# Edge tiles of 121 rows instead of 125, ids transposed on the chip, and another order of TensorE's products in the mixer of a graph layer

## The reference, cut to what matters

```python
xn = layernorm(x)
# graph attention: el, er (N, 8) are logits of source and target, feat_v (N, 8, 64) the values
e = leaky_relu(el[src] + er[dst], 0.2)
a = softmax of e over the edges of each dst (segment max, exp, segment sum)
gnn[dst] += a * feat_v[src]                       # segment sum over 100000 edges
# mixer: linear attention with positive random features
q, k, v = heads(xn @ Wq)/8, heads(xn @ Wk)/8, heads(xn @ Wv)
phi(t) = max(exp(-|t|^2/2), 1e-8) * exp(min(t @ omega, 50))
mix = (phi(q) @ (phi(k).T @ v)) / (phi(q) @ sum phi(k)) @ Wo
x1 = x + gnn + mix
# routed part: gates, 8 Sinkhorn rounds, top 781 rows of each of 8 experts, one product each
out = x1 + combine(experts(layernorm(x1)))
```

## Time and profile before

| | us |
|---|---|
| median of three runs | 3183.67 (3181.99 to 3190.54) |
| the profiled execution | 3169.73 |
| its span | 3167.7 |
| TensorE busy | 2547.4 (80%) |
| GpSimd busy | 2208.5 (70%) |
| VectorE busy | 1620.6 (51%) |
| ScalarE busy | 992.5 (31%) |
| mean granted TensorE clock | 0.92 of full speed |

### The profile page before, as it was taken

One profiled execution on the slowest core, in us unless ns is written; L12 is line 12 of the kernel. 1 busy time (PEld: TensorE's weight loads), 2 busy tenths in 40 slices (PEclk: granted clock), 3 DMA queues, 4 the chain that ended last, 5 costly groups with the idle time before them and its releaser, 6 DMA issues.

```text
span 3167.7 us, 47560 instructions
## 1 busy us (share of the span) xinstructions
PE 2547.4 (80%) x10463; PEld 1775.2 (56%) x10464; DVE 1620.6 (51%) x2963; ACT 992.5 (31%) x2564; POOL 2208.5 (70%) x1847
## 2 busy tenths in 40 slices
PE   6699999999999979941776777777788888824998
PEld 3377766667766644421554556666666666723443
DVE  6622222222222279986744555565666666767232
ACT  2322222222222200020544545554555556600111
POOL 6477777877777877787877777777777777500454
PEclk9899999999999999975799999998999999956999
DMA  6531111111111133321666677777777777630111
GB/s 162 143 81 30 29 29 30 32 29 29 29 29 29 24 118 115 115 57 24 164 173 175 178 184 182 179 183 175 188 189 195 192 194 200 174 110 0 45 52 39
DMA packets 276634, 341.25 MB, mean 108 GB/s; under 512 B 165456, under 2 KB 184631, under 8 KB 276451
## 3 DMA queue, kind: packets, MB, share of 16 engines
q0 software_dynamic: 218672, 227.51, 32.0%
q1 hardware_dynamic: 52093, 93.57, 9.4%
q10 hardware_dynamic: 5810, 19.52, 2.0%
HBM read 285.65 MB, written 55.25 MB: 108 GB/s over the span
## 4 chain that ended last, share of the span: by engine, by line
POOL 41%; issue 16%; PE 15%; DMA 14%; DVE 9%; DVEq 3%; POOLq 0%; ACT 0%
POOL R L554 31%; PE ps L642 14%; DMA R<-val_tab,src_i 13%; POOL R L596 8%; POOL er_starts L567 2%; DVEq L240 1%; DVEq L1469 1%; DVE work L1563 1%; DVE R L1469 1%; PE ps L939 1%; DVE work L1229 1%; PE ps L667 1%; DVE work L1239 0%; DVE R L1450 0%; DVE work L1509 0%
## 5 line engine op out<-in xcount | busy, mean ns | idle before, releaser
L642 PE MATMUL ps<-R,work 125*125 (+3 forms) x5240 | 1639.7, 467 | 254.5 <-DVE R L1469 229.9
L642 PEld LDWEIGHTS ps<-R,work 125*125 125x125 f32 (+2 forms) x5240 | 978.9, 194 | 821.1 <-issue 689.2
L554 POOL DMA_INDIRECT R<-el_tab,src_i x800 | 985.6, 1232 | 323.6 <-issue 284.1
L596 POOL DMA_INDIRECT R<-val_tab,src_i x800 | 979.2, 1224 | 284.9 <-issue 185.6
L1469 DVE TENSOR_TENSOR R<-R,ps (+1 forms) x800 | 520.5, 692 | 131.7 <-DVE ps L1458 125.8
L1119 ACT ACTIVATE work<-work 125x125 f32<-125x125 f32 x900 | 277.8, 309 | 492.3 <-PE ps L642 464.2
L642 PE MATMUL ps<-work,R 128*128 128x250 f32 x1600 | 359.1, 383 | 21.9 <-DMA work<-R 21.9
L1116 ACT ACTIVATE work<-work,negdst 125x125 f32<-125x125 f32 x900 | 353.6, 393 | 73.9 <-issue 52.0
L642 PEld LDWEIGHTS ps<-work,R 128*128 128x128 f32 x1600 | 308.6, 194 | 59.1 <-issue 22.0
L1458 DVE COPY ps<-R (+1 forms) x401 | 69.7, 174 | 306.7 <-POOLq L602 233.1
L1301 DVE TENSOR_TENSOR R<-ps,R 125x512 f32<-125x512 f32 x50 | 34.6, 691 | 357.6 <-PE ps L642 357.6
(11 more groups left out here) (256 smaller groups left out, 2173.5 us busy)
## 6 DMA issues: line engine op xcount, KB each, us to landing
R<-el_tab,src_i POOLq DMA_INDIRECT x800
R<-val_tab,src_i POOLq DMA_INDIRECT x800, 6.0
val_tab<-R SPq DMA_DIRECT2D x50, 253.9 KB
work<-R SPq DMA_DIRECT2D x25, 500.0 KB, 3.6
work<-xm_tab SPq DMA_DIRECT2D x50, 250.0 KB
out_dram<-R SPq DMA_DIRECT2D x50, 250.0 KB
work<-in_x_dram SPq DMA_DIRECT2D x17, 500.0 KB
xm_tab<-work ACTq DMA_DIRECT2D x17, 500.0 KB
```

The source lines that it names most:

```text
L554: eng.indirect_dma_start(out=ELP[:, g, c, :], out_offset=None, in_=el_tab[:, :], in_offset=bass.IndirectOffsetOnAxis(ap=src_i[:, t:t + 1], ...
L596: eng.indirect_dma_start(out=ring[:, slot, :], out_offset=None, in_=val_tab[:, :], in_offset=bass.IndirectOffsetOnAxis(ap=src_i[:, 2 * u + ...
L642: return pe.matmul(o, l, r, start=start, stop=stop)
```

## The change

Edge tiles have R = 121 rows: 827 would do, made even to 828; 52 places to a chunk in place of 50, the last chunk has 48. All tables of edges (src_i, dst, weights, er_starts, scans) take that size: 16 x 52 x 121 = 100672 places, of which the last are blank. FIRST goes from 11 to 12, R2 is 384 columns wider.

As `srcT` and `dstT` are laid out for 125 rows, the ids are laid out anew on the chip. dst is read from its flat form, 128 rows of 121 at a time, cast to float, and turned by TensorE into `negdst`. src is loaded as `srcT`, turned back into rows, written flat to HBM (`src_flat`), read in rows of 121, and turned again, by TensorE behind x groups 0 and 1. `dst_i` and its load are gone; er and its bias have a tensor of their own.

In the mixer TensorE takes v before vg, and the first of four q chunks between the two `scores_k`. VectorE joins two operations (a maximum and a product) into one in two places.

```diff
-CL = E // NCH
-CT = CL // P
+R = 121
+TIL = 2 * -(-E // (2 * R))
+CT = -(-TIL // NCH)
+LT = NCH * CT
+LAST = TIL - (NCH - 1) * CT
+CL = CT * R
+EP = NCH * CL
+LW = LT * 8
-FIRST = 11
+FIRST = 12
-R1W, R2W = 26024, 16384
+R1W, R2W = 26024, 16768
...
 SP:
-            for g in range(NXI):
+            eng.dma_start(id_col.bitcast(INT32), srcT).then_inc(S["ids_loaded"], 16)
+            load_x(0)
+            eng.wait_ge(S["ids_made"], 1)
+            eng.dma_start(id_dst[:, 0:TG, :].bitcast(INT32), spread_rows(dst, R)).then_inc(S["ids_loaded"], 16)
...
+            for g in range(1, NXI):
                 load_x(g)
...
-                    eng.wait_ge(S["v_psum"], used)
+                    eng.wait_ge(S["vg_psum"], used)
...
 GpSimd:
-            eng.dma_start(src_i[:, :], srcT).then_inc(S["idx_loaded"], 16)
             eng.wait_ge(S["row_ready"], 2)
+            eng.memset(ELP[:, LAST:CT, NCH - 1, :], 0.0).then_inc(S["tables_ready"], 1)
             eng.wait_ge(S["el_written"], 16 * G)
-            eng.wait_ge(S["idx_loaded"], 16)
+            eng.wait_ge(S["ids_made"], 7)
...
-                    for c in range(NCH):
+                    for c in range(NCH if g < LAST else NCH - 1):
...
-            for u in range(ET // 2):
+            for u in range(TIL // 2):
...
 TensorE:
+            def turn_loaded_ids():
+                pe.wait_ge(S["ids_made"], 4)
+                pe.wait_ge(S["xnT_ready"], 1)
+                for k in range(TG + 1):
+                    w_ = min(128, ET - 128 * k)
+                    last = pe.transpose(ps[0:w_, k // 4, (k % 4) * P:(k % 4) * P + P], id_col[:, 128 * k:128 * k + w_], ident[0:P, 0:P])
+                last.then_inc(S["ids_turned"], 1)
+                pe.wait_ge(S["ids_made"], 5)
+                pe.wait_ge(S["xnT_ready"], 2)
+                turn_ids(R, id_dst, LT, 2).then_inc(S["ids_turned"], 1)
+
+            def turn_sources():
+                pe.wait_ge(S["src_moved"], 80)
+                pe.wait_ge(S["ids_kept"], 3)
+                turn_ids(R, id_src, TIL, 0).then_inc(S["ids_turned"], 1)
...
+                    if isinstance(g, int) and g == 2:
+                        pe.wait_ge(S["ids_made"], 7)
+                    if isinstance(g, int) and g == 3:
+                        pe.wait_ge(S["negdst_ready"], 1)
                     turn(g, b)
                     if isinstance(g, int) and g == 1:
+                        turn_loaded_ids()
                         spread_params()
+                        turn_sources()
...
                 def values(j):
+                    pe.wait_ge(S["v_copied"], 2 * g + j)
+                    ... v product into bank 3, v_psum
                     pe.wait_ge(S["vg_read"], 2 * g + j)
                     ... vg product into bank 2, vg_psum
-                    pe.wait_ge(S["v_copied"], 2 * g + j)
-                    ... v product into bank 3, v_psum
...
                 scores_k(0)
+                queries(0)
                 scores_k(1)
-                for c in range(C):
-                    for k in range(KC):
-                        last = mm(chunk(0, c, 0, GT), w_q[:, k, 128 * c:128 * c + 128], xT[b][:, k, :], k == 0, k == KC - 1)
+                for c in range(1, C):
+                    last = queries(c)
...
 ScalarE, behind copy_xT(1):
+            def keep_ids():
+                act.wait_ge(S["ids_turned"], 2)
+                ... three copies of the turned src to id_row
+                act.wait_ge(S["ids_kept"], 3)
+                ... two DMAs id_row -> src_flat
+                act.wait_ge(S["ids_turned"], 3)
+                ... two copies of the turned dst, times -1, to negdst
+                act.wait_ge(S["src_moved"], 32)
+                ... three DMAs src_flat -> id_src
...
 VectorE:
+            def keep_sources():
+                v.wait_ge(S["ids_turned"], 4)
+                v.tensor_copy(src_i[:, 0:512], ps[0:R, 0, :]).then_inc(S["ids_made"], 1)
+                v.tensor_copy(src_i[:, 512:TIL], ps[0:R, 1, 0:TIL - 512]).then_inc(S["ids_made"], 1)
...
                         fold_logit_weights()
+                        keep_sources()
+            v.memset(id_dst[:, TG, :].bitcast(INT32), N).then_inc(S["ids_made"], 1)
+            v.memset(id_src[:, TG, :], 0.0).then_inc(S["ids_made"], 1)
             first_tile()
             stats(0, 0, 0)
+            v.wait_ge(S["ids_loaded"], 64)
+            v.tensor_copy(id_col, id_col.bitcast(INT32)).then_inc(S["ids_made"], 1)
+            v.tensor_copy(id_dst, id_dst.bitcast(INT32)).then_inc(S["ids_made"], 1)
+            first_slot()
             trip(0)
...
-                    st.done(v.tensor_scalar(nk[0:P, j, :], nk[0:P, j, :], EPS_PHI, None, ALU.max))
-                    v.tensor_tensor(out=p3, in0=p3, in1=nk[0:P, j, :].unsqueeze(2).to_broadcast([P, H, F]), op=ALU.mult)\
-                        .then_inc(S["phi_ready"], 1)
+                    v.scalar_tensor_tensor(out=p3, in0=nk[0:P, j, :].unsqueeze(2).to_broadcast([P, H, F]), scalar=EPS_PHI, in1=p3,
+                                           op0=ALU.max, op1=ALU.mult).then_inc(S["phi_ready"], 1)
...
-            v.wait_ge(S["heads_in"], 64)
-            v.tensor_scalar(negdst[:, :], dst_i[:, :], -1.0, None, ALU.mult).then_inc(S["negdst_ready"], 1)
```

More of the change, by code:

```diff
@@ L22 @@
 NCH = 16
-CL = E // NCH
-CT = CL // P
+R = 121
[6 more added lines that the diff above has]
+LW = LT * 8
+assert TIL % 2 == 0 and 0 < LAST <= CT
+TG = TIL // 128
+TREM = TIL - 128 * TG
 X = 8
@@ L66, in block_tiles @@
 def block_tiles(k):
-    return NCH * (min(TB * k + TB, CT) - TB * k)
+    return sum(NCH if g < LAST else NCH - 1 for g in range(TB * k, min(TB * k + TB, CT)))
 def logits_by(k):
@@ L182, in gps_layer @@
         rcnt_ = rcnt[:, :]
[L183 to L187, removed]
+        EWLO = R2W - LW
+        EW = R2[0:R, EWLO:R2W].rearrange("p (t h) -> p t h", h=H)
+        EW2 = R2[0:R, EWLO:R2W].rearrange("p (u h) -> p u h", h=2 * H)
+        WS = [R2[:, LW + 2048 * i:LW + 2048 + 2048 * i].rearrange("p (k n) -> p k n", k=KC) for i in range(4)]
         w_vg, w_k, w_v, w_q = WS
@@ L521, in _ @@
             eng.sem_inc(S["consts_ready"], 1)
[L522 removed]
+            for t_ in (ident[:, :], halves[:, :], half2[:, :], before[:, :]):
                 st.done(eng.memset(t_, 0.0))
@@ L608, in _ @@
                     report(u - BEHIND)
-            for u in range(ET // 2 - BEHIND, ET // 2):
+            for u in range(TIL // 2 - BEHIND, TIL // 2):
                 report(u)
@@ L727, in values @@
                 def values(j):
+                    pe.wait_ge(S["v_copied"], 2 * g + j)
+                    for k in range(KC):
+                        last = mm(ps[0:P, 3, :], xT[b][:, k, j * P:j * P + P], w_v[:, k, :], k == 0, k == KC - 1)
+                    last.then_inc(S["v_psum"], 1)
                     pe.wait_ge(S["vg_read"], 2 * g + j)
@@ L819, in turn_block @@
                 for g in range(TB * k, min(TB * k + TB, CT)):
-                    last = pe.transpose(ps[:, b, (g % TB) * P:(g % TB) * P + P], tab_[:, g - first, :, :].rearrange("p c h -> p (c h)"),
-                                        ident[0:P, 0:P])
+                    last = pe.transpose(ps[:, b, (g % TB) * R:(g % TB) * R + R], tab_[:, g - first, :, :].rearrange("p c h -> p (c h)"),
+                                        ident[0:R, 0:R])
                 last.then_inc(S["seg_t_psum"], 1)
@@ L1007, in trip @@
                         load_x(g + NXI, b)
+                    if isinstance(g, int) and g == 1:
+                        keep_ids()
                     if not isinstance(g, int) or g >= 1:
@@ L1324, in trip @@
                 v.wait_ge(S["qexp_done"], 2 * g + 2)
-                st.done(v.tensor_scalar(ts2, ts2, EPS_PHI, None, ALU.max))
-                v.tensor_tensor(out=xnT_all[:, :, bass.ds(g * GT, GT)], in0=ts3, in1=ts23, op=ALU.mult).then_inc(S["phiq_ready"], 1)
+                v.scalar_tensor_tensor(out=xnT_all[:, :, bass.ds(g * GT, GT)], in0=ts23, scalar=EPS_PHI, in1=ts3,
+                                       op0=ALU.max, op1=ALU.mult).then_inc(S["phiq_ready"], 1)
             trips(v, G, trip)
-            st.end(G)
             v.wait_ge(S["kv_added"], G)
```

179 lines of the change are left out of this document (107 added, 72 removed).

## The result

The changed kernel needs 4281.55 us (median of 4 runs, 4278.23 to 4301.12), the kernel before 3182.83 beside it: a ratio of 1.3465, 95% interval 1.3413 to 1.3517. 3060 was forecast. In a later session, on a chip with the number 11, the same program needs 2995.98 us against 3166.85, a ratio of 0.9461 (0.9411 to 0.9511). (The chip of the first session is not known.) So two results have to be explained; their traces agree to within 4 us up to the first mixer product (161.7 us and 158.0).

The account below looks back on a forecast made before the run. GpSimd's gathers were taken to set the pace from 138 us on; +4 -37 -28.5 +1 -59 = -119.5 on 3169.7 gave 3050, raised to 3060 for the runs' higher median; range 3005 to 3175 (this case 3015 to 3115).

Parts of the forecast that it names:

- The price of a gather: GpSimd's logit and value gathers: 121 rows cost 1.040 us, with 0.30 us of issue a pitch of 1.34 us.
- Rivals B: All gathers: odd rows cost, not the split; 1.14 us each, pitch 1.44, together -11 us, 3169; chance 0.08.
- Rival C: All gathers: any row count not a multiple of 16 costs 1.20 us; +85 us, 3264; chance 0.09.
- law of rows per engine: Gathers: cost follows each DMA engine's share of rows, 23 ns per row from 1 to 7, 11.6 ns from 7 to 25.
- Step 1: LayerNorm: the new id work delays the first half by +4 us, bounds 0 and +25.
- D: LayerNorm: the id chain stalls it by 25 us or more; 3080 us and up, inside the range; no separate chance.
- Step 2: Mixer: the new order of products fills TensorE's two waits per group, -37 us, bounds 0 and -38.
- Step 3: Logit gathers: 94 us shorter, so GpSimd is 31 us early and the wait for it goes, -28.5 us.
- Second half: Value gathers and messages: -59 us; VectorE is the bound from block 18 on, GpSimd's 62 us of landing waits kept.
- rival A: Second half: landings become the bound, GpSimd's 62.6 us of waits for them double; 3120 us, chance 0.15.

Follow-up runs that it names:

- run 5: The kernel before with each logit gather fetching 121 of its tile's 125 rows, value gathers left at 125: 3124.33 us beside 3163.84.
- Run 1: The changed kernel with tiles of 125 rows again, everything else of the change kept: 3154.27 us beside 3148.14 for the kernel before.

## Why the prediction was right or wrong

The kernel was forecast 4% faster and measured 35% slower. By stages, in the spans (starts of the first mixer product, the last L1308/L1406, the first copy of L1386/L1480, the first and last message): the kernel before, and against it the changed kernel in the crawl and on chip 11.

| | before | crawl | chip 11 | forecast of the step |
|---|---|---|---|---|
| up to the mixer | 157.1 | +4.6 | +0.9 | +4 |
| mixer to its last k scores | 938.8 | +954.9 | -54.9 | -37 |
| rest of it and attention | 275.9 | -8.2 | -8.2 | 0 |
| from there to the first message | 160.8 | -28.2 | -27.1 | -28.5 +1 |
| messages | 1232.2 | +182.4 | -85.0 | -59 |
| tail | 402.9 | +5.6 | -0.3 | 0 |
| span | 3167.7 | +1111.1 | -174.5 | -119.5 |

The trace of the kernel before is one execution of 3169.73 us, the same for both columns. It is not known on which chip it was taken; its time lies among those beside the runs without a crawl. Between the medians on chip 11 the gain is 170.9 us. The -8.2 us in the third row were not forecast and not looked into.

- **The price of a gather** was right. Medians by rows: 125 (5x25) 1.203 to 1.211 us, 121 (11x11) 1.022 (1.014 in run 5), 110 (11x10) 1.009, 120 (15x8) 0.986, 128 (16x8) 0.947; the pitch for 121 is 1.327 us against 1.34 forecast. Rivals B (1.14) and C (1.20) fall. More engines are cheaper even at the same eight rows each (0.986 and 0.947), which the forecast's law of rows per engine alone does not have. The Trainium skill's rule ("DMA: Bandwidth & Descriptors", section "Why a DMA increments its semaphore by 16 and not by 1") fits the order of these five prices. It is not enough alone: the 112-row gathers of the routed part, which by it have 16 engines too, cost 0.993 to 1.000 us, more than 120 and 128 rows. So the smooth curve from 16 over 112 to 125 rows, on which the forecast rests, gave the right price for 121, in part by luck. That 128 rows would be better still could have been read from that curve (16x8, 1.006 us by the same law, and 782 gathers in place of 828).
- **Step 1** (+4): right, +4.6 in the crawl, +0.9 on chip 11. The id chain stayed covered; D falls.
- **Step 2** (mixer, -37, bounds 0 and -38) is the step that failed, in both directions. On chip 11 it gave 17.9 us more than forecast. Over the whole stretch the two waits were 21.4 and 17.6 us, 39.0 together, and none is left; the other 15.9 us are TensorE's own busy time, 899.8 before and 883.9 after for the same products, a term that I had put at nothing. Some 9 of them are the clock, by my estimate: from 175 us to the last k scores the granted clock was 0.99 before and is 1.00 after, and 1% of the 882 us busy there is 9. The rest was not separated. In the crawl the step is +954.9. The bounds took it that TensorE's speed in the mixer does not depend on how GpSimd issues its gathers; every row that I read of it was taken at a pitch of 1.505 us. No rival carried it: all of them looked for the price of a gather on GpSimd, its landings or the waits of the new code. Rival C has the sign, by another mechanism (a dear gather), and 85 of the 1111 us. In its place the runs showed that in some sessions the stream of gathers itself starves TensorE, ScalarE and VectorE of their issue: 74 matmuls in 200 us and not 885.
- **Step 3** (logit gathers, wait for them gone): right. TensorE's 35.8 us for el_tab are gone in both; GpSimd's last logit gather starts at 1353.4 us on chip 11, its first value gather 41 us later, so GpSimd is early by that (31 forecast). Run 5 has the same from the other side: with 121 rows alone the start moves by 39 us. Run 1 bears out, in one execution, that the mixer's gain is worth nothing while GpSimd is the bound.
- **Second half** (-59, with the 62 us of waits for landings kept): mechanism right, size off by 26. GpSimd's and VectorE's waits on chip 11, 1530 to 2570 us, against the earlier trace rows:

```profile
DVE ps L1552 <- POOLq L630: 131.1, 116, 7.1
...
POOL R L624 <- PE ps L670: 49.3, 109, 3.0
...
POOL R L624 <- DMA R<-val_tab,src_i: 40.1, 51, 3.8
```

  VectorE waits 131 us for GpSimd and not 233, as forecast, and GpSimd waits 40.1 us for landings and not 62.6: that can be 22 of the 26, if each of these waits was on the path. Landings became quicker (below, against 6.0), so rival A falls, and with it what I drew there from the Trainium skill on five shared engines (nor would 11 of 16 engines always meet a given five: the other eleven are free of them).

```profile
DMA to landing us min/median/max: 3.9/4.8/11.9
```

  In the crawl the stage loses 182 us; I take it for a milder form of the same thing, which is argued and not shown. Waits there from 2550 to 3840 us:

```profile
POOL R L624 <- PE ps L670: 292.9, 128, 8.5
...
PE ps L670 <- ACT work L1204: 144.6, 94, 3.2
DVE R L1563 <- issue: 140.7, 241, 2.6
ACT work L1204 <- remote: 136.7, 61, 3.7
```

  Now GpSimd waits for TensorE, TensorE for ScalarE, and ScalarE and VectorE for "issue" and "remote". Each such wait of GpSimd breaks the row of back-to-back gathers, which may be why it is mild; that was not tried.
- **The sum.** Without the crawl it is 64 us too high (2996 against 3060, and just under the low end of the range, 3005): 18 from the mixer, 26 from the messages, 8 from the third row, 3 from LayerNorm, and the 10 us put on for the gap between profile and median, which did not carry over. In the crawl nothing in the range's high end stands for what happened. The range also has a slip: 3060 + 20 + 37 + 21 is 3138, not 3115.

## What to carry to other kernels

Choose the rows of an indirect gather so that they split evenly over many engines: 128 rows and not 125, with the rest of this change, took 272 of 3167 us on chip 11, with ratios of 0.914 to 0.915 in three comparisons, and beat the 121 rows by 102 us; on chip 14 they lost 28%. But before a faster stream on GpSimd is trusted, time it on several chips, each time with the kernel before and the changed kernel beside the variant: the same program was 5% faster on one and 35% slower on another, and without the changed kernel as a control the first eight runs here could not tell a cure from a chip. Where a trace shows engines idle on "issue" in even steps with low DMA, look at what GpSimd issues at that time, and not at the waits.

## What the runs showed of the hardware that was not expected

- In some sessions, back-to-back gathers every 1.25 us (128 rows) or 1.33 us (121 rows) stall TensorE, ScalarE and VectorE: TensorE in steps of 1.400 us with holes up to 67.7 us, VectorE's starts 67.2 and 112.0 us apart at the same places. Scatters of 125 rows every 1.49 us or more in the same traces do not. Pitch and number of engines are not told apart.
- GpSimd's own gathers keep their pace in that state: with 121 rows 1.022 us in the median and a pitch of 1.327 us, with the crawl and without.
- A gather of 128 rows costs GpSimd less (0.947 us) than one of 110 (1.009 us) or of 112 (0.994 us, another gather of the same kernel).
